# Zero writes on GpSimd between the row sends at the end of the first graph stage

## What is computed

```python
x = x + _L0_gnn_ref(_layernorm(x), adj, ...)   # graph attention, 4 heads, sigmoid scores
x = x + _L0_ffn_ref(_layernorm(x), ...)        # experts: 2 of 8 for each node
x = x + _L1_gnn_ref(_layernorm(x), adj, ...)   # graph attention by exponentials
x = x + _L1_ffn_ref(_layernorm(x), ...)        # experts: 2 of 8 for each graph
```

```python
h = gelu(einsum('td,edh->teh', xf, W1) + b1)
y = einsum('teh,ehd->ted', h, W2) + b2
out = einsum('ted,te->td', y, mask)
```

## Time and profile before

| | |
|---|---|
| median of 3 runs | 715.46 us (711.8 to 718.67) |
| the profiled execution | 714.54 us, its span 712.7 us |
| mean granted clock of TensorE | 0.93 |
| busy share of the span: PE, PEld, DVE | 89%, 74%, 72% |
| busy share: ACT, POOL | 66%, 50% |
| row sends (L1269) | 64, 65.3 us of GpSimd |
| result scatters (L1951) | 91, 87.4 us of GpSimd |

### The profile page before, as it was taken

How to read it: one execution, slowest core, us unless ns; L and a number is a source line. 1 busy time by engine, 2 the same in 40 slices (tenths; PEclk the granted TensorE clock), 3 DMA queues, 4 the chain that set the end, 5 groups by cost and what they waited for, 6 DMA issues and landing times. The chain is left out here.

```text
span 712.7 us, 18377 instructions
## 1 busy us (share of the span) xinstructions
PE 636.5 (89%) x5323; PEld 525.3 (74%) x5323; DVE 511.3 (72%) x2246; ACT 471.8 (66%) x1286; POOL 356.2 (50%) x603
## 2 busy tenths in 40 slices
PE   7799999999999756697999999996789889999993
PEld 5555566666566435696999999996788878999993
DVE  6899999999999768354444444443899941778898
ACT  6678999998998533344666666672257767666661
POOL 2144546878778762443444454545542105755540
PEclk9999999999999755698999999996999968999997
DMA  6357243543221113211664454315893101022011
GB/s 184 112 127 169 75 121 109 153 137 126 92 80 65 38 38 119 55 53 48 164 154 123 134 159 142 93 55 108 185 267 120 60 0 61 1 90 61 31 60 59
DMA packets 75795, 71.79 MB, mean 101 GB/s; under 512 B 7782, under 2 KB 64770, under 8 KB 74930
## 3 DMA queue, kind: packets, MB, share of 16 engines
q1 hardware_dynamic: 62194, 51.12, 24.9%
q0 software_dynamic: 11200, 13.35, 7.8%
q10 hardware_dynamic: 2304, 6.16, 3.0%
HBM read 44.06 MB, written 26.54 MB: 99 GB/s over the span
## 5 line engine op out<-in xcount | busy, mean ns | idle before, releaser
L1951 POOL DMA_INDIRECT expert_outputs<-y_rows,y_at x91 | 87.4, 960 | 96.9 <-DVE y_rows L1922 91.5
L1713 ACT ACTIVATE hT<-psum,b1blk 128x128 f32<-128x128 f32 x280 | 79.9, 369 | 42.1 <-issue 30.8
L1629 PE MATMUL psum<-xinT,w1blk 128*128 128x128 f32 x728 | 101.3, 284 | 6.5 <-ACT xinT L1698 6.2
L1629 PEld LDWEIGHTS psum<-xinT,w1blk 128*128 128x128 f32 x728 | 93.1, 200 | 7.8 <-ACT xinT L1698 6.9
L1651 PE MATMUL psum<-f_w,hT 128*128 x728 | 98.4, 280 | 0.0
L1651 PEld LDWEIGHTS psum<-f_w,hT 128*128 128x128 f32 x728 | 90.9, 196 | 0.1
L1269 POOL DMA_INDIRECT pair_rows<-rows,row_of x64 | 65.3, 1020 | 32.2 <-DVE row_of L1050 19.0
L1903 DVE TENSOR_SCALAR w1blk<-f_w 128x256 f32 x182 | 46.8, 299 | 44.9 <-issue 44.0
L908 DVE TENSOR_TENSOR adj_h<-psum,adjT 128x1024 f32<-128x1024 f32 x64 | 75.5, 1217 | 2.0 <-ACT psum L687 1.9
L687 ACT ACTIVATE psum<-psum 128x1024 f32<-128x1024 f32 x64 | 64.2, 1008 | 13.5 <-PE psum L431 10.4
L1922 DVE TENSOR_TENSOR y_rows<-psum,b2wide 128x128 f32<-128x128 f32 x91 | 26.5, 292 | 63.9 <-PE psum L1651 50.1
(11 more groups left out here) (369 smaller groups left out, 1508.0 us busy)
## 6 DMA issues: line engine op xcount, KB each, us to landing
adj_in<-in_adj_dram SPq DMA_DIRECT2D x32, 256.0 KB
adjT_scratch<-adjT SPq DMA_DIRECT2D x32, 256.0 KB
adjT<-adjT_scratch SPq DMA_DIRECT2D x6, 1024.0 KB
xin<-pair_rows SPq DMA_DIRECT2D x91, 64.5 KB
xres<-in_x_dram SPq DMA_DIRECT2D x16, 256.0 KB, 4.5
b2wide<-b_of_blocks ACTq DMA_DIRECT2D x7, 512.0 KB
xres<-expert_outputs POOLq DMA_DIRECT2D x6, 512.0 KB, 9.5
out_dram<-yout SPq DMA_DIRECT2D x6, 512.0 KB, 3.7
```

What stands on the lines that cost most here:

```text
L1629: ins = nc.tensor.matmul(psum[:, HIDDEN_BANKS + n % 2, lo:lo + P], w1blk[:, u, k, c * P:(c + 1) * P], xinT[:, u, :], start=True, stop=True)
L1713: ins = nc.scalar.activation(hT[:, u, k, c, :], psum[:, HIDDEN_BANKS + n % 2, lo:lo + P], ACT.Gelu, bias=first_bias[:, c, k, i:i + 1])
L1951: pool.indirect_dma_start(y_dram[:, :], bass.IndirectOffsetOnAxis(ap=y_at[:, u:u + 1], axis=0), y_rows[:, u, :], None).then_inc(s_y_sent[u ...
```

## The change

Behind every send that `send_group` issues, GpSimd gets a write of zeros over two thirds of the tile `w_all` (128 partitions x 256 float32). The writes count up a semaphore of their own, `s_apart`, and each waits for the write before it. A result scatter (L1951) gets none. This makes 24 writes: 8 in group 5, 8 in group 6, 4 in group 7, 4 in group 8. The lists of PE, DVE, ACT and SP hold what they held.

```diff
+        s_apart = sem("s_apart")
...
+            pauses = itertools.count()
+
+            def keep_apart(n):
+
+                if n > 0:
+                    pool.wait_ge(s_apart, n)
+                nc.gpsimd.memset(w_all[:, 0:2, :], 0.0).then_inc(s_apart, 1)
+
             def send_group(g, parts=None):
                 for part in parts or range(ROUTES[g][1]):
-                    send(g, part)
+                    for t in range(TB):
+                        send(g, part, [t])
+                        keep_apart(next(pauses))
```

## The result

The changed kernel takes 708.39 us (median, 705.06 to 711.41) and the kernel before, beside it, 712.48 (710.55 to 718.67). The ratio is 0.9928, 95% interval 0.9911 to 0.9946. That is 5.1 us of 712.5; the two medians are 4.1 apart. Predicted were 705 us, 9.8 less, in a range of 696 to 720. The sign is the forecast's, the size is about half of it.

The account below looks back on a forecast made before the run. TensorE, busy 89% of the span, was taken to wait for late news during close GpSimd sends. Hand-overs 5.9 + clock 2.9 + shorter holes 2 - ring 1 = 9.8 us off 714.54: 705 us, range 696 to 720.

Parts of the forecast that it names:

- falling to about 1 us each: Sign of the mechanism: remote waits of ACT and DVE in the three runs of sends, then 3.97, 3.55, 4.55 and 6.93 us.
- The writes' own time: On GpSimd: 0.31 us a write, sends every 1.42 us (or 1.57), adding 3.8 to 7.4 us to GpSimd.
- Group 5 and its cover: Before the last output: 1.5 of 3.5 us gained; some 5 us before TensorE takes SP's first loads cover group 5's delay.
- Groups 6 and 7: Blocks 0 to 3: hand-overs about 1 us late each, 2.0 of 6.0 us gained, plus half of 3.9 us of clock.
- Whatever TensorE gains there reaches the end, since its later blocks are dense.: Step carrying all TensorE gains in the runs of groups 5 to 8, at most 20.6 us, through to the kernel's end.
- Group 8: Behind group 8's sends: about three hand-overs still 1 us late, 2.4 of 5.4 us gained, plus half of 1.8 us of clock.
- the ring: Ring of eight results: scatters queued behind group 8's later sends hold DVE up, 0.6 to 1.2 us, counted as 1 lost.
- All of it: Upper bound if pauses let every increment through at once: 3.5 + 6.0 + 5.4 + 3.9 + 1.8 = 20.6 us.
- Contention with DVE: Zero writes holding DVE instructions up: 7.4 us of DVE if every write did, 0 on the path, 1 as bound.
- the lateness lasts as long as the run: Rival, runs of sends: news comes only behind the longer run, so the time is 719.3 to 723 us; chance 0.2.
- the write hides in the 0.30 us of issue: Part of the no-change rival, on GpSimd: spacing stays near 1.26 us and so does the time; within its chance 0.25.
- The sends are not the cause: No-change rival: late news comes from something else in these stretches, pauses cost 0 to 2 us, 714.5 to 716.5; chance 0.25.

Follow-up runs that it names:

- single-group kernels: Zero writes behind the sends of group 5, of groups 6 and 7, or of group 8 only, against the kernel before: ratios 0.9991, 0.9987, 1.0006.
- the third comparison: Kernel before at 690.10 us; against it scatters in fours 0.9984, changed kernel with fours and writes 1.0040, with group 4's pauses 1.0010, with all pauses 1.0062.
- the bursts: Scatters of blocks 28 to 83 issued in fours: kernel before plus this 689.61 us; changed kernel plus this and a write behind each 693.53 us.
- the first two comparisons: Two comparisons of four follow-up kernels each against the kernel before, which took 714.88 us in one and 714.37 us in the other.

## Why the prediction was right, and where it was too large

*Right: the mechanism and its places, in a comparison where news came late.* Remote waits shrank where the pauses were put, TensorE's holes behind them too, and the clock came back (0.52 to 0.88, 0.70 to 1.00). Each of the single-group kernels shows it for the waits of its group, none of them in the time. The forecast's own sign, waits "falling to about 1 us each", came only in group 5.

*Luck.* That the change met such a comparison was luck: in the third, kernels with these pauses and more came out at 1.001 to 1.006. The range of 696 to 720 took in no change as well. The forecast gave 0.45 to a gain of over 1% and 0.1 to a smaller one, and 0.7% is a smaller one. It also called 1% the least that can be told from no change; the interval reached 0.2% to either side.

*The writes' own time* was taken as 0.31 us and a spacing of 1.42. It is 0.33 and mostly 1.46:

```profile
258.03 0.33 POOL L1306 MEMSET w_all<- 128x256 f32 x1
258.52 0.96 POOL L1270 DMA_INDIRECT pair_rows<-rows,row_of  x1 [0.17 <-issue]
...
259.98 0.97 POOL L1270 DMA_INDIRECT pair_rows<-rows,row_of  x1 [0.17 <-issue]
```

*Group 5 and its cover.* 1.5 us was forecast and 1.87 came, at block 0; so close a fit is partly chance, with 3.0 us between two profiles of the same pauses. SP's first loads begin at 270.42 for 270.02 before, not at 271 to 273, so the cover held.

*Groups 6 and 7* were to give 2.0 by shorter hand-overs, 2.0 of clock (half of 3.9) and 2 by shorter holes elsewhere, 6.0 in all. Blocks 0 to 5 give 7.75, but blocks 5 to 12 take 3.23 back, 4.5 net. **This is the step that failed: "Whatever TensorE gains there reaches the end, since its later blocks are dense."** The blocks are dense behind 345 in these two profiles, but for waits of 1.03 us and less, not between 292 and 312. There block 5, which had run behind the sends, now runs beside the stretched end of them. TensorE stands for 2.08 us before 294.34, for a copy by DVE that is behind the late reader of 292.62 in DVE's list; what took the rest of the 3.23 isn't shown:

```profile
294.34 1.15 PE L1640 MATMUL psum<-xinT,w1blk 128*128 128x128 f32 x8 [2.08 <-DVE w1blk L1914]
```

*Group 8* was to give 2.4 for the hand-overs and 0.9 of clock, less 1 for the ring, 2.3. Blocks 12 to 20 give 1.87. The three hand-overs, taken as about 1 us late each, were the weak part: the news of blocks 8 and 9 is 2.9 and 5.7 us late, and two remote waits of over 3 us are left in this run,

```profile
315.57 0.28 ACT L1709 ACTIVATE xinT<-psum 128x128 f32<-128x128 f32 x1 [4.10 <-remote]
...
319.36 0.29 DVE L1933 TENSOR_TENSOR y_rows<-psum,b2wide 128x128 f32<-128x128 f32 x1 [3.34 <-remote]
```

while GpSimd goes from the last sends, 1.46 us apart, to scatters that got no pause and follow one another at 1.27 us.

Against the profile the sum is then 1.87 + 4.52 + 1.87 + 0.21 = 8.5 for 9.8. The rest of the miss, 8.5 to 5.1, is the difference between one execution of each and the medians: in this comparison the two were on opposite sides. A forecast that is made against one profile carries that.

*"All of it" was put at 20.6 us.* The third comparison has a measure of it, the same order without late news in one profile: 24.6. A part that I had not counted is the wait of 3.1 us at 242.

*Contention with DVE* was taken as 0 on the path. That fits the time, but not for the reason that the prediction took from the Trainium skill. The copies of L1903 took 296 ns each from 277 to 345 before and 341 (L1914) after, and 293 against 388 in the bursts. The Trainium skill ("SBUF — State Buffer", Who interferes with whom) has this in another sentence than the one I weighed: `tensor_scalar` is named among the operations that can take the port pair that DVE shares with GpSimd. By that, a zero write can meet them, and the traces agree.

*The rivals.* That the lateness lasts as long as the run, and makes it slower, is refuted for a spacing of 1.46 in the time, though more hand-overs were late than before. That the write hides in the 0.30 us of issue is what one element does (spacing 1.27, ratio 0.9994), not what 256 do. "The sends are not the cause" had two parts. In the first two comparisons the late waits moved with the spacing, whatever was put in between, with the exception of group 5 under the one-element write. But the third shows that close sends alone don't make them: they have a part in it, with something else that these traces don't name. So my theory holds only where that is present. There the sentence of the Trainium skill ("SBUF — State Buffer", Who interferes with whom) that "PE and ACT never wait on anyone", which is about ports, doesn't cover ACT's remote waits; in the third comparison no row read here speaks against it.

## What to carry to other kernels

A wait with producer and consumer long ready is a delay on the way and not work. Find it by the producer's end and the reader's start, not by the mark "remote" alone, which missed some here. Then look at what another engine issues in an unbroken row at that time, and change the time between, not the kind, of these instructions. Before such a repair is kept, measure it in more than one comparison: here it gave 0.7% (with group 4 and the scatters 1.8%) where the lateness was present, and where it was absent three kernels with these pauses and more were between no slower and 0.6% slower. And time won in one stretch counts only from where the engine is dense; between the hole and that point the next blocks can meet the same wait.

## What was not expected of the hardware

- News from TensorE came to DVE 6.0 and 6.5 us late while GpSimd's indirect transfers followed one another at 1.26 us, 2.9 to 5.7 late with sends at 1.46, and on time in groups 5 to 7 at 1.83; and in another comparison, with the same instructions and the same spacing, never late in the one profile of it. The median of one kernel was 714 us there and 690 here.
- The traces with late news hold 8112 to 8328 records of semaphore updates, those without 11023 to 11083, of kernels that differ by at most 80 GpSimd instructions.
- A write of 256 float32 a partition takes GpSimd 0.33 us, one of 16 columns 0.13, one of 1 element 0.11; in front of a transfer, either of the small ones all but hides in its issue (sends 1.27 to 1.28 us apart, 1.26 without).
- With a write behind nearly every scatter, DVE's copies of 128x256 take 388 ns each on average in place of 293.
